# A two-pass scan and Fourier-weight kernel: the scan's product moved in pass B, preparation spread over more slots, states copied in half as many DMAs

## What is computed

```python
xn = (x - mu) / jnp.sqrt(var + LN_EPS) * ln_gamma + ln_beta
delta = jax.nn.sigmoid(jnp.einsum('btd,ds->bts', xn, w_delta) + b_delta)
B_t = jnp.einsum('btd,ds->bts', xn, w_in) + b_in
gate = jax.nn.sigmoid(jnp.einsum('btd,de->bte', xn, w_gate) + b_gate)
def step(h, inp):
    d_t, b_t = inp
    h_new = jnp.tanh(h * d_t @ A + b_t)      # 16 states
    return (h_new, h_new)
...
y = jnp.swapaxes(jnp.einsum('tbs,se->tbe', hs, C), 0, 1) * gate
return y + x
# and around it
x = _layernorm(x + _L0_attn_ref(x, ...), axis=-1)
x = _layernorm(x + _L0_ffn_ref(x, ...), axis=-1)   # fft, product with w, real part of ifft, + bias
```

## Time and profile before

| | us |
|---|---|
| median of 3 runs | 936.36 (933.77 to 939.24) |
| the profiled execution | 937.29 |
| its span, first to last instruction | 935.5 |
| PE busy | 869.6 |
| DVE busy | 747.9 |
| POOL busy | 575.0 |
| ACT busy | 555.7 |

### The profile page before, as it was taken

How to read it: one execution, slowest core, us unless ns; L and a number is a source line. 1 busy time by engine, 2 the same in 40 slices (tenths; PEclk the granted TensorE clock), 3 DMA queues, 4 the chain that set the end, 5 groups by cost and what they waited for, 6 DMA issues and landing times.

```text
span 935.5 us, 16634 instructions
## 1 busy us (share of the span) xinstructions
PE 869.6 (93%) x5100; PEld 455.1 (49%) x5100; DVE 747.9 (80%) x1515; ACT 555.7 (59%) x1059; POOL 575.0 (61%) x906
## 2 busy tenths in 40 slices
PE   7999999998999999988888888889999999999997
PEld 4454445444455555544444444444445555555553
DVE  7888888899998888966777777779768888888883
ACT  3344444533444444534456666669768888878887
POOL 3656666687555565555555555557567777767772
PEclk8999999999999999998999999999999999999998
DMA  7579888776665668755444553456867766677753
GB/s 292 185 257 316 314 313 297 257 245 226 211 240 195 211 192 304 244 177 211 165 150 162 173 204 137 158 172 218 248 231 236 266 233 222 235 254 247 240 188 135
DMA packets 94446, 209.52 MB, mean 224 GB/s; under 512 B 4016, under 2 KB 5296, under 8 KB 90416
## 3 DMA queue, kind: packets, MB, share of 16 engines
q1 hardware_dynamic: 94096, 208.49, 64.7%
q10 hardware_dynamic: 288, 0.27, 0.1%
HBM read 139.53 MB, written 67.11 MB: 221 GB/s over the span
## 4 chain that ended last, share of the span: by engine, by line
PE 61%; DVE 16%; issue 7%; POOL 5%; ACT 5%; DMA 3%; SPq 1%; DVEq 0%; POOLq 0%; ACTq 0%
PE bank L1415 15%; PE bank L1416 15%; PE bank L1418 15%; PE bank L1405 6%; PE bank L1501 4%; DVE zh_sb L1080 3%; DVE w_ring L1309 3%; DVE gate_sb L1298 2%; ACT hi_sb L666 2%; POOL lo_sb L742 2%; PE bank L1567 2%; DVE bn L1162 1%; SPq L443 1%; DVE xs_sb L1194 1%; PE bank L1481 1%
## 5 line engine op out<-in xcount | busy, mean ns | idle before, releaser
L742 POOL TENSOR_TENSOR lo_sb<-xs_sb,hi_sb 128x512 f16<-128x512 f32 x128 | 152.0, 1187 | 159.1 <-ACT hi_sb L527 159.1
L1415 PE MATMUL bank<-wg_hi,hi_sb 128*128 128x512 f16 x512 | 196.5, 384 | 15.0 <-DVE gsum_sb L1209 9.6
L818 POOL TENSOR_TENSOR x_sb<-x_sb,gate_sb 128x512 f32<-128x512 f32 x120 | 152.7, 1273 | 76.3 <-DMA x_sb<-x 60.2
L1415 PE MATMUL bank<-w_re_sb,hi_sb 128*128 128x512 f16 x512 | 195.4, 382 | 1.8 <-DVE w_ring L1309 1.5
L1416 PE MATMUL bank<-wg_lo,hi_sb 128*128 128x512 f16 x512 | 196.3, 383 | 0.0
L1416 PE MATMUL bank<-w_re_sb,hi_sb 128*128 128x512 f16 x512 | 195.5, 382 | 0.0
L527 ACT ACTIVATE hi_sb<-xs_sb 128x512 f16<-128x512 f32 x128 | 80.5, 629 | 177.6 <-DVE xs_sb L1194 173.9
L1199 DVE SCALAR_TENSOR_TENSOR lo_sb<-bank,hi_sb 128x512 f16<-128x512 f32 x128 | 88.5, 691 | 90.4 <-ACT hi_sb L666 89.4
L1418 PE MATMUL bank<-wg_hi,lo_sb 128*128 128x512 f16 x512 | 133.6, 384 | 0.0
L1418 PE MATMUL bank<-w_re_sb,lo_sb 128*128 128x512 f16 x512 | 132.3, 381 | 0.0
L674 ACT ACTIVATE norm_sb<-x_sb,lift_bias,rstd 128x512 f32<-128x512 f32 x128 | 103.1, 805 | 22.5 <-POOL lift_bias L831 19.5
(11 more groups left out here) (184 smaller groups left out, 1392.1 us busy)
## 6 DMA issues: line engine op xcount, KB each, us to landing
x_sb<-x SPq DMA_DIRECT2D x63, 1024.0 KB, 6.2
gate_dram<-gate_sb SPq DMA_DIRECT2D x32, 1024.0 KB, 5.2
out<-out_sb SPq DMA_DIRECT2D x31, 1024.0 KB, 5.3
gate_sb<-gate_dram SPq DMA_DIRECT2D x30, 1024.0 KB, 7.0
out_sb<-x_turned SPq DMA_DIRECT2D x16, 1024.0 KB, 7.3
norm_sb<-x_turned SPq DMA_DIRECT2D x15, 1024.0 KB, 7.2
w_ring<-gate_dram SPq DMA_DIRECT2D x2, 1024.0 KB, 9.5
x_sb<-x SPq DMA_DIRECT2D x2, 512.0 KB, 5.4
```

The source lines that it names most:

```text
L742: pool.tensor_tensor(lo_sb[:, k % 4], xs_sb[:, k % 2], hi_sb[:, k % 4], ALU.subtract).then_inc(s_lo, 1)
L818: pool.tensor_tensor(x_sb[:, k // 4, k % 4], x_sb[:, k // 4, k % 4], gate_tile(n, k), ALU.add).then_inc(s_v, 1)
L1415: nc.tensor.matmul(dst, hi_sb[:, slot_of, t], w_hi[:, t], start=(t == 0), stop=False)
```

## The change

Five edits, none of which adds or takes away arithmetic.

1. In pass B DVE's `scan_slot(1, n)` stands between the statistics and the low half, in place of the slot's end. `state_low` becomes a `split_slot` of its own and stays at the end of the slot (in pass A it stands where it did).
2. `count_changes` goes from the start of PE's slot to its end, `scan_flag` and the branch one slot later, and the split one slot later with them (pass A: last `state_low` in slot 109, before in 108; pass B: in slot 44, before in 43).
3. `combine` goes from the end of DVE's slot n+1 into slot n+2, behind `scaled`; `combined_high` and `combined_low` go to n+3; `pq_sb` gets a second buffer, `bias_rep`.
4. `PREPARATION` runs over slots 42 to 79, and the folds of POOL stand in slots with n mod 4 of 2 or 3, where no `row_statistics` and no `token_diagonal` is.
5. The states go into `h_rep` in 8 DMAs of 128 KB for a group, four and four: the first four stand **between** the two halves of octet 13 (pass A) or octet 5 (pass B) in SP's list, behind the wait for the split; the others after the second half.

```diff
-SCAN_BRANCH = tuple(n + 2 for n in SCAN_CHECK)
+SCAN_BRANCH = tuple(n + 3 for n in SCAN_CHECK)
+ROW_FOLDS, COLUMN_FOLDS = (50, 51, 54, 55, 58, 59, 62, 63), (66, 67, 70, 71)
+WEIGHTS_HIGH = (68, 69, 72, 73)
...
+        pq_ring = (pq_sb[:], bias_rep[:])
...
-            def replicate_states(g):
-                for r in range(BATCH // 2):
-                    first = g * ROWS + r % 2 * 32
-                    for seg in range(4):
-                        src = (h_hi, h_hi, h_lo, h_lo)[seg]
-                        sp.dma_start(h_rep[32 * seg:32 * seg + 32, r, g * GROUP:(g + 1) * GROUP],
-                                     src[first:first + 32, r // 2]).then_inc(s_hrep[g][r], 16)
+            def replicate_states(g, odd):
+                first = g * ROWS + odd * 32
+                for seg in range(4):
+                    src = (h_hi, h_hi, h_lo, h_lo)[seg]
+                    sp.dma_start(h_rep[32 * seg:32 * seg + 32, odd::2, g * GROUP:(g + 1) * GROUP],
+                                 src[first:first + 32]).then_inc(s_hrep[g][odd], 16)
...
                 second_pass(v, 0)
+                if v == 5:
+                    sp.wait_ge(s_split[1], 1)
+                    replicate_states(1, 0)
                 second_pass(v, 1)
-            sp.wait_ge(s_split[1], 1)
-            replicate_states(1)
+            replicate_states(1, 1)
...
-                if isinstance(n, int) and 52 <= n < 60:
-                    fold_rows(n - 52)
-                if isinstance(n, int) and 60 <= n < 68 and n % 2 == 0:
-                    fold_columns((n - 60) // 2)
+                if isinstance(n, int) and n in ROW_FOLDS:
+                    fold_rows(ROW_FOLDS.index(n))
+                if isinstance(n, int) and n in COLUMN_FOLDS:
+                    fold_columns(COLUMN_FOLDS.index(n))
...
-                48: prepare_scan, 50: prepare_biases, 52: sum_weights, 55: copy_sums, 56: scale_of_w,
...
+                42: prepare_scan, 43: scale_bias, 46: largest_c, 50: sum_weights, 51: largest_bias,
...
+                if isinstance(n, int) and pair_at(n - 2) is not None:
+                    combine(pair_at(n - 2))
                 if k % 4 == 1 and exists(n + 3):
                     token_inverse((k + 3) // 4 % 2)
...
                     b_statistics(n + 4, (k + 4) % 8)
                     dve.wait_ge(s_bbn, n + 5)
+                scan_slot(1, n)
                 if exists(n + 1):
                     low_half(n + 1, k + 1, s_bhi, s_blo)
...
-                scan_slot(1, n)
+                split_slot(1, n)
```

More of the change, by code:

```diff
@@ L358, in build @@
         s_split = [sem(f"scan_split{g}") for g in range(2)]
-        s_hrep = [[sem(f"h_rep_loaded{g}_{r}") for r in range(BATCH // 2)] for g in range(2)]
+        s_hrep = [[sem(f"h_rep_loaded{g}_{odd}") for odd in range(2)] for g in range(2)]
         s_hbefore = sem("state_before_second_group")
@@ L648, in slot @@
                     delta(v - 1)
[L649 to L652, removed]
+                if isinstance(n, int) and 46 <= n < 50:
+                    sum_weights(n - 46)
+                if isinstance(n, int) and n in WEIGHTS_HIGH:
+                    frequency_weights_high(WEIGHTS_HIGH.index(n))
                 split_slot(0, n)
@@ L655, in slot @@
                     copy_even(pair_at(n - 1))
-                if isinstance(n, int) and pair_at(n - 2) is not None:
-                    combined_high(pair_at(n - 2))
+                if isinstance(n, int) and pair_at(n - 3) is not None:
+                    combined_high(pair_at(n - 3))
             def b_hi(n, k):
@@ L984, in scale_c, with split_c @@
                 unscales(2, 3, 2 * STATE_SCALE)
-            def split_c():
-                wait_own(nc.vector.tensor_scalar(c_hi[:], c_rep, scale[:, 2:3], None, ALU.mult))
+            def split_c(low):
+                if not low:
+                    wait_own(nc.vector.tensor_scalar(c_hi[:], c_rep, scale[:, 2:3], None, ALU.mult))
+                    return
                 wait_own(nc.vector.scalar_tensor_tensor(c_lo[:], c_rep, scale[:, 2:3], c_hi[:], ALU.mult,
@@ L1284, in slot @@
                 scan_slot(0, n)
+                split_slot(0, n)
                 if isinstance(n, int) and n in PREPARATION:
                     PREPARATION[n]()
-                if isinstance(n, int) and pair_at(n - 1) is not None:
-                    combine(pair_at(n - 1))
             def gated(n, k, v):
@@ L1527, in scan_slot, with check_slot @@
                     scan_step(g, at[0] * CHUNK + at[1] + 1, at[1])
+                if isinstance(n, int) and n == SCAN_BRANCH[g]:
+                    scan_until_settled(g)
+            def check_slot(g, n):
                 if isinstance(n, int) and n == SCAN_CHECK[g]:
@@ L1555, in states_out @@
             def states_out(n, k, v):
-                if isinstance(n, int) and n < 8 and n % 2 == 0:
+                if isinstance(n, int) and n in (0, 2):
                     pe.wait_ge(s_hrep[0][k // 2], 4 * 16)
                 if isinstance(n, int) and n == 8 * B_WRITTEN + 6:
-                    for r in range(BATCH // 2):
-                        pe.wait_ge(s_hrep[1][r], 4 * 16)
+                    for odd in range(2):
+                        pe.wait_ge(s_hrep[1][odd], 4 * 16)
                 if isinstance(n, int) and n == 0:
```

44 lines of the change are left out of this document (24 added, 20 removed).

## The result

The changed kernel takes 898.83 us in the median of 4 runs (897.09 to 900.27), the kernel before 935.07 (931.97 to 939.24). The ratio is 0.9609, 95% interval 0.9564 to 0.9654. The profiled executions took 937.29 and 897.09, 40.2 apart; the medians are 36.2 apart, since the profiled execution of the kernel before is slower than its median and that of the changed kernel is the fastest of its four.

A forecast was written before the change was run, and what follows sets the result against it. DVE's order, not its sum, was taken to set the pace of pass B's scanned slots. Terms 28.2 + 7.5 - 4.0 + 6.5 + 2 = 40.2 took 937.3 to 897.1, less 0.9 for the median: 896 us, range 885 to 909.

The forecast's parts named there:

- the loop: Pass B scan: moving the product ahead of the low half cuts slots from 4.68 to 3.80, gaining 28.2 us.
- the end of pass A: End of pass A: with fewer copies ahead of the norm_sb load, its stall and slow clock go, 7.5 us gained.
- the preparation: Preparation slots of pass A: moved folds and earlier DVE instructions save 6.5 us, bounds 2 and 11.
- combine and check: Later combine no longer waits for ACT's copy, later check no longer holds PE: together 2 us, from -2 to 4.
- a floor of 3.76: Pass B scanned slots: PE's own work of 3.25 plus a scan step of 0.51; 29.4 us gained if reached.
- The rivals of edit 1: Pass B scan: longer products, 906 (chance 0.09) or 917 (0.05); no gain, 924 (0.04); slower, 993 (0.02).
- products near 0.39: Sign in pass B's scanned slots: DVE's product L1091 would last near 0.39 us, with DVE idle ahead for the tanh.
- The two rivals built on longer products, 906 and 917: Pass B scan: every product lasts 1.32, time 906, chance 0.09; or waits a whole residual, time 917, chance 0.05.
- my price: End of pass A: four copies and h_before hold SP's list for 3.2 us by the copy, 6.5 by bytes.
- The stall of pass B: Pass B, after the scan: loads behind the split and copies come late, a 6 to 9 us stall; net -4.0.
- I let a half go: Preparation slots of pass A: of 12.5 us counted as preparation, about half would be saved, taken as 6.5.
- term 4: Pass B: SP's loads wait behind a split one slot later and four copies; net -4.0 us, from -8 to +1.

The follow-up runs named there:

- `copies_behind`: The changed kernel with all eight copies of group 1 in pass B behind both halves of octet 5 on SP's queue: 891.04 us, ratio 0.9523.
- The two narrow kernels: The kernel before with POOL's folds of the weights, or DVE's wide preparation instructions, cut to 8 columns: 934.01 and 931.25 us, one run each.

## Why the prediction was right, and where not

The forecast was 896 in a range of 885 to 909; the median is 898.83. The main mechanism was right, and it makes 30.5 of the 36.2. That the number fits so well is in part luck. Two terms were too small (the loop and the end of pass A), two too large (the preparation, combine and check), and they made up for each other: with what the runs show for each, the sum is 37 to 38. And the forecast sum of 40.2 is the very difference of the profiled executions only because the one lay above its median and the other below; the medians are 36.2 apart.

1. **The loop through the product.** Right in its mechanism: edit 1 alone gives 30.5, all but edit 1 leaves 4.70 a slot. The forecast was 28.2 at 3.80 a slot, with a floor of 3.76. The slot is 3.69 to 3.71, below that floor. The mis-sized piece is the scan step: I read 0.51 for it from a slot in which PE had stood before it; without the wait it is 545.54 - 545.12 = 0.42, and the floor is 3.25 + 0.42 = 3.67.
2. **The rivals of edit 1.** I had said that POOL's residual is mostly over before the next product, and wanted products near 0.39. That reading failed. The product did get longer, as the rule on the lock would have it:

```profile
L1091 DVE TENSOR_TENSOR zh_sb<-h_sb,del_sb x60: 347/742/1346, 241.1 to 575.8; 64x128 f32<-64x128 f32 x60
```

   The median is 742 ns against 388, the longest 1.35 against 1.32, and none reaches 1.66. These rows hold both passes; in pass B alone the median goes from 384 to 772 and the longest from 1.08 to 1.34. PE set the pace all the same, since DVE's slot with a product of 1.14 still ends in time. What the Trainium skill states there (SBUF — State Buffer, "SBUF: two separate sides") agrees with 546.24, where the product lasted until 547.38 and POOL's residual until 547.13. It agrees with all others too: in both traces each product that lasted longer than 0.45 (14 of 30 in pass B before, 19 of 30 after) had started beside a running POOL instruction and ended 0.22 to 0.25 after it. The two rivals built on longer products, 906 and 917, did not come.
3. **The end of pass A.** Forecast 7.5. From gate_logits 112 to ffn_sum 0 the traces take 61.5 and 52.5, 8.9 gained. Five other kernels without edit 5 take 60.0 to 62.2 there. The four with edit 5 and without edit 2 take 53.3, the four with both 52.5, so 0.8 of the gain comes with edits 2 and 3, and 7.5 is not outside what edit 5 gives. Neither end of my price was met: four copies and `h_before` held SP for 4.6 (399.45 to 404.04), against 3.2 by the copy and 6.5 by bytes, nearer the first.
4. **The stall of pass B.** Forecast -4.0, with 6 to 9 us for the wait and 1.7 for the clock; measured -3.9, with a wait of 5.18 for the gate, more behind it for `x`, and 3.4 us at the lower clock. The mechanism is what was foreseen, and `copies_behind`, without the stall, takes 891.04 where I had named about 890. That the two figures meet to 0.1 is luck: against the other three traces of the same pass B (55.8 to 58.2) the loss would be 4.4 to 6.8.
5. **The preparation.** Forecast 6.5, measured 1.4. The step that failed is "I let a half go": no row said that half of the 12.5 us was the cost of a bad order. The two narrow kernels show that 4.7 goes with most of the work itself on either engine, and POOL's part of the move is worth 1.5 alone. PE's wait of 3.5 for diagonals is gone, as foreseen. Another wait rose: DVE's for the mean square, which is 7.5 in the changed kernel, was before:

```profile
DVE token_pow L1167 <- POOL mean_square L728: 4.2, 6, 1.1
```

6. **Combine and check.** Forecast 2, measured 0 (ratio 0.9997). The step that failed: a wait of DVE was counted as time. It went, and DVE's wait for the mean square grew by 3.9 in its place, while the 40 slots stayed as long. Edit 2 has a price besides, that I had put into term 4: together with edit 5, one slot later for the split adds 3 us to the wait for the gate in pass B (2.1 against 5.2).

Left open: through which wait the places of DVE's table within four slots are worth 2 us, whether the two times 4.7 of the narrow kernels add up, and what the rest of the 12.5 us is; and how the gain at the end of pass A divides between fewer copies and their earlier place.

## What to carry to other kernels

Where an engine at 93% still waits at the same instruction in every slot, follow that wait once around; if it closes through an in-order queue, try moving one instruction ahead in that queue. Here that gave 30.5 us in pass B and 3.5 in pass A, with no work taken away. A wait on SP's list belongs behind the loads that the next units need; in pass B splitting the batch of copies in two cost time, since the first half brought the wait with it. Don't cost a move of preparation by what the stretch loses: leave the moved work out in a trial, of all engines at once, and take what that gives as the bound.

## What the runs showed that I had not expected

- In pass B a step of two small float32 products costs PE 0.42 us when it follows other products (0.41 to 0.43 in 28 steps and more of each of three traces) and 0.50 to 0.51 when PE stood before it (30 steps of the kernel before). In pass A most steps without a wait take 0.48 or 0.49; why is not shown.
- DVE's product became twice as long in the median of pass B (772 against 384 ns) in a kernel that is 36 us faster: it moved to a place where POOL is busy, and had room there.
- A copy of 128 KB between SBUF tiles holds SP's queue hardly longer than one of 64 KB (597 and 590 ns at least; 0.97 and 0.76 us each in a row in pass A, 0.71 and 0.71 in pass B).
